# Lane-major q/k columns in fewer, longer loads, and the query mask added in the row-maximum pass

## The reference

```python
x = x + _L0_attn_ref(_layernorm(x), ...)
x = x + _L0_ffn_ref(_layernorm(x), ...)
x = x + _L1_attn_ref(_layernorm(x), ...)
x = x + _L1_ffn_ref(_layernorm(x), ...)
# _L1_attn_ref
q = jnp.einsum('btc,oc->bto', x, Wq).reshape(B, T, H, D)
k = jnp.einsum('btc,oc->bto', x, Wk).reshape(B, T, H, D)
v = jnp.einsum('btc,oc->bto', x, Wv).reshape(B, T, H, D)
att = jnp.einsum('bqhd,bkhd->bhqk', q, k) * SCALE
att = jnp.where(mask[None, None, :, :], -jnp.inf, att)   # mask: j > i
att = jax.nn.softmax(att, axis=-1)
out = jnp.einsum('bhqk,bkhd->bqhd', att, v).reshape(B, T, C)
return jnp.einsum('btc,oc->bto', out, Wo)
```

## Time and profile before

| | us |
|---|---|
| median of 3 runs | 2110.64 |
| range of the runs | 2103.11 to 2110.79 |
| the profiled execution | 2108.77 |
| its span | 2107.0 |

### The profile page before, as it was taken

How to read it: one execution, slowest core, us unless ns; L and a number is a source line. 1 busy time by engine, 2 the same in 40 slices (tenths; PEclk the granted TensorE clock), 3 DMA queues, 4 the chain that set the end, 5 groups by cost and what they waited for, 6 DMA issues and landing times.

```text
span 2107.0 us, 34513 instructions
## 1 busy us (share of the span) xinstructions
PE 1619.2 (77%) x10136; PEld 907.4 (43%) x10136; DVE 1236.6 (59%) x3717; ACT 778.5 (37%) x1387; POOL 501.6 (24%) x487
## 2 busy tenths in 40 slices
PE   3869898979787878888888888798889781137765
PEld 2335454535353434444444444444454441135554
DVE  5456767666667575757575757575766526861111
ACT  1225252525252525252525252525254242134331
POOL 2311212121212121212121212121212002006887
PEclk7879999989899989899989899999999875568897
DMA  2041321313131313130313130404031400024444
GB/s 63 16 50 33 40 50 27 50 26 51 25 52 25 52 24 57 19 59 18 58 18 59 17 61 15 64 12 63 13 58 20 65 7 10 0 39 86 89 89 59
DMA packets 113452, 86.56 MB, mean 41 GB/s; under 512 B 21569, under 2 KB 107841, under 8 KB 113345
## 3 DMA queue, kind: packets, MB, share of 16 engines
q1 hardware_dynamic: 102080, 76.58, 21.4%
q0 software_dynamic: 11264, 8.92, 3.2%
HBM read 58.95 MB, written 25.72 MB: 40 GB/s over the span
## 4 chain that ended last, share of the span: by engine, by line
PE 47%; DVE 17%; issue 17%; POOL 5%; DMA 4%; ACT 4%; SPq 2%; DVEq 1%; ACTq 0%; POOLq 0%
PE ba L580 6%; PE bo L839 5%; PE facc L695 5%; PE fa L669 5%; PE ba L585 5%; PE fa L685 5%; POOL out L552 3%; SPq L330 2%; ACT probs L1015 2%; DVE passed L1460 2%; DVE nm L1263 2%; PE ba L587 2%; PE ba L582 2%; POOL got L522 2%; DMA KT<-qk_parts 1%
## 5 line engine op out<-in xcount | busy, mean ns | idle before, releaser
L585 PE MATMUL ba<-KT,QT 72*128 72x512 bf16 (+3 forms) x1024 | 262.2, 320 | 182.5 <-DVE nm L1263 129.2
L1015 ACT ACTIVATE probs<-ba 128x512 f32<-128x512 f32 x640 | 330.5, 640 | 97.7 <-PE ba L582 96.9
L459 POOL TENSOR_TENSOR hh<-th,gb 128x512 f32<-128x512 f32 x128 | 161.9, 1265 | 697.5 <-ACT gb L971 427.0
L580 PE MATMUL ba<-QT,KT 75*128 75x512 bf16 (+3 forms) x1024 | 253.3, 310 | 35.2 <-ACT probs L1015 28.7
L1263 DVE TENSOR_REDUCE nm<-ba 128x1 f32<-128x512 f32 x256 | 174.6, 682 | 179.5 <-issue 131.2
L585 PEld LDWEIGHTS ba<-KT,QT 72*128 72x128 bf16 x1024 | 105.0, 103 | 344.5 <-DVE nm L1263 155.8
L587 PE MATMUL ba<-mask_q,identb 128*128 128x128 bf16 x1024 | 200.8, 230 | 0.0
L987 ACT ACTIVATE sil<-fa 128x512 f32<-128x512 f32 x160 | 95.4, 596 | 274.9 <-PE fa L669 274.8
L582 PE MATMUL ba<-mask_k,identb 128*128 128x128 bf16 x1024 | 195.5, 224 | 0.0
L669 PE MATMUL fa<-f_nT,w 128*128 128x512 f32 x320 | 187.1, 669 | 1.2 <-ACT sc L1046 1.2
L685 PE MATMUL fa<-f_nT,w 128*128 128x512 f32 x320 | 181.1, 649 | 0.0
(11 more groups left out here) (284 smaller groups left out, 2643.2 us busy)
## 6 DMA issues: line engine op xcount, KB each, us to landing
QT<-qk_parts SPq DMA_DIRECT2D x288, 64.0 KB
KT<-qk_parts SPq DMA_DIRECT2D x288, 64.0 KB
qk_parts<-qkp SPq DMA_DIRECT2D x32, 384.0 KB, 2.5
fc<-in_L_ffn_fc_weight SPq DMA_DIRECT2D x32, 256.0 KB
xin<-in_L_attn_x SPq DMA_DIRECT2D x16, 256.0 KB, 13.4
out<-x SPq DMA_DIRECT2D x16, 256.0 KB, 2.3
xn_rows<-row SPq DMA_DIRECT2D x16, 256.0 KB, 2.4
w<-in_L_w SPq DMA_DIRECT2D x3, 640.0 KB, 6.7
```

The lines of the kernel that those rows point to most:

```text
L459: pool.tensor_tensor(hh[:, e % 2], th[:, e % 2], gb[:, e % 2], ALU.mult).then_inc(S["s_h"], 1)
L580: pe.matmul(bank[:, col:col + w], lhsT=KT[0:K_ROWS, head, blk * P:(blk + 1) * P], rhs=QT[0:K_ROWS, head, blk * P:], start=True, stop=False)
L585: pe.matmul(bank[:, col:col + w], lhsT=QT[0:QK_ROWS, head, blk * P:(blk + 1) * P], rhs=KT[0:QK_ROWS, head, 0:w], start=True, stop=False)
L1015: act.activation(probs[:, pair % 3, f_], ba[n % 3][:], ACT.Exp, scale=SCALE).then_inc(S["s_exp"], 1)
```

## The change

The weights of q and k are copied once into `w_qk` with their columns in lane-major order, d * 16 + h, so that the 16 heads of a lane are neighbours in q, k and `qk_parts`. `qk_parts` gets 5 slots for parts instead of 3; for k, slots 3 and 4 are parts 0 and 1 again, written by one more DMA. The 72 rows of `QT` and `KT` are taken in three shifts of 24: q parts 0, 1, 2 against k parts shift, shift + 1, shift + 2, so one load fills 24 partitions, with a run of 8 heads of 512 tokens, 8 KB, for each. There are 12 loads per batch instead of 36, and the totals that the semaphores wait for are adapted.

`mask_q` becomes 512 wide, zero but for the last 128 columns. The second matmul of a query-major fill goes. VectorE's reductions become `tensor_tensor_reduce`: negated (scores + mask), written back into the PSUM bank, and their minimum, started from 1e38, into `nm`. A fill with two heads takes two such operations instead of one, and each fill's first stands behind a separate wait and no-op (`apart`).

```diff
-        qk_parts = nc.dram_tensor("qk_parts", (BATCH, 2, PARTS, P, SEQ), BF16, kind="Internal").ap()
+        qk_parts = nc.dram_tensor("qk_parts", (BATCH, 2, 2 * PARTS - 1, P, SEQ), BF16, kind="Internal").ap()
...
-                    sp.dma_start(qk_parts[b, w].rearrange("c p t -> p c t"), qkp[:, w]).then_inc(S["s_qkw"], 16)
-                sp.wait_ge(S["s_qkw"], 32 * b + 32)
+                    sp.dma_start(qk_parts[b, w].rearrange("c p t -> p c t")[:, 0:PARTS], qkp[:, w]).then_inc(S["s_qkw"], 16)
+                sp.dma_start(qk_parts[b, 1].rearrange("c p t -> p c t")[:, PARTS:], qkp[:, 1, 0:PARTS - 1]).then_inc(S["s_qkw"], 16)
+                sp.wait_ge(S["s_qkw"], 48 * b + 48)
...
-                for i in range(PARTS):
-                    for j in range(PARTS):
-                        r = (i * PARTS + j) * HD
-                        for t, w, part in ((QT, 0, i), (KT, 1, j)):
-                            sp.dma_start(t[r:r + HD, heads], qk_parts[b, w, part].rearrange("(h d) t -> d h t", d=HD)[:, heads])\
-                              .then_inc(S[f"s_qk{half}"], 16)
+                for shift in range(PARTS):
+                    r = slice(shift * PARTS * HD, (shift + 1) * PARTS * HD)
+                    for t, w, part in ((QT, 0, 0), (KT, 1, shift)):
+                        rows = qk_parts[b, w, part:part + PARTS].rearrange("c (d h) t -> (c d) h t", h=HEADS)
+                        sp.dma_start(t[r, heads], rows[:, heads]).then_inc(S[f"s_qk{half}"], 16)
...
             const(pool.memset(mask_q[:], 0.0))
-            const(pool.affine_select(mask_q[:], mask_q[:], [[-1, P]], ALU.is_ge, MASKED, base=0, channel_multiplier=1))
+            last_ = mask_q[:, SEQ - P:]
+            const(pool.affine_select(last_, last_, [[-1, P]], ALU.is_ge, MASKED, base=0, channel_multiplier=1))
...
-                    pe.matmul(bank[:, col:col + w], lhsT=QT[0:QK_ROWS, head, blk * P:(blk + 1) * P],
-                              rhs=KT[0:QK_ROWS, head, 0:w], start=True, stop=False)
-                    last = pe.matmul(bank[:, col + w - P:col + w], lhsT=identb[:], rhs=mask_q[:], start=False, stop=True)
+                    last = pe.matmul(bank[:, col:col + w], lhsT=QT[0:QK_ROWS, head, blk * P:(blk + 1) * P],
+                                     rhs=KT[0:QK_ROWS, head, 0:w], start=True, stop=True)
...
-                pe.matmul(facc[:], lhsT=w_q1[:], rhs=b_nT[:], start=True, stop=True).then_inc(S["s_q"], 1)
+                pe.matmul(facc[:], lhsT=w_qk[:, 0].rearrange("p d h -> p (d h)"), rhs=b_nT[:], start=True, stop=True).then_inc(S["s_q"], 1)
...
                 dve.wait_ge(S["s_S"], FILLS * b + n + 1)
+                apart(dve)
+
+                def lowest(head, blk, col):
+
+                    w = (blk + 1) * P
+                    return dve.tensor_tensor_reduce(bank[:, col:col + w], bank[:, col:col + w], mask_q[:, SEQ - w:], -1.0, -MASKED, ALU.add, ALU.min,
+                                                    nm[:, blk, head:head + 1])
+
                 if f in (0, 2):
-                    last = dve.tensor_reduce(nm[:, 3, h:h + 1], bank[:], X, ALU.max, negate=True)
+                    last = lowest(h, 3, 0)
                 elif f in (1, 3):
-                    dve.tensor_reduce(nm[:, 2, h:h + 1], bank[:, 0:384], X, ALU.max, negate=True)
-                    last = dve.tensor_reduce(nm[:, 0, h:h + 1], bank[:, 384:512], X, ALU.max, negate=True)
+                    lowest(h, 2, 0)
+                    last = lowest(h, 0, 384)
                 else:
-                    last = dve.tensor_reduce(nm[:, 1, h:h + 2], bank[:].rearrange("p (h k) -> p h k", h=2), X, ALU.max, negate=True)
+                    lowest(h, 1, 0)
+                    last = lowest(h + 1, 1, 256)
...
+                    for w, t in enumerate((w_q1, w_k1)):
+                        dve.tensor_copy(w_qk[:, w], t[:].rearrange("p (h d) -> p d h", d=HD)).then_inc(S["s_wqk"], 1)
```

More of the change, by code:

```diff
@@ L74, in build_kernel @@
         identb = sb("identb", [P, P], BF16)
-        mask_q = sb("mask_q", [P, P], BF16)
         mask_k = sb("mask_k", [P, P], BF16)
@@ L88, in build_kernel @@
         logits_flat = sb("logits", [P, TILES, E1])
+        mask_q = sb1("mask_q", [P, SEQ], BF16)
         w_kvq = sb1("w_kvq", [P, 3 * D])
@@ L104, in build_kernel @@
         w_v1 = sb1("w_v1", [P, D])
+        w_qk = sb1("w_qk", [P, 2, HD, HEADS])
         w_o1 = sb1("w_o1", [P, D])
@@ L243, in build_kernel @@
             s_h1 s_h3 s_gb s_gbc s_sil s_t s_h s_hs s_ym s_yT s_yTt s_x2 s_fc
-            s_pad s_lnb s_varb s_rsb s_T3 s_nT3 s_q s_k s_v s_p1 s_r1 s_p2 s_p3 s_vp s_qkw s_qk0 s_qk1 s_S s_red s_nmp s_nmt
+            s_pad s_wqk s_lnb s_varb s_rsb s_T3 s_nT3 s_q s_k s_v s_p1 s_r1 s_p2 s_p3 s_vp s_qkw s_qk0 s_qk1 s_S s_red s_nmp s_nmt
             s_nmT s_mx0 s_mx1 s_st s_exp s_pv s_oT s_tr s_norm s_aTt s_aT s_wo s_x3 s_row s_T4 s_nT4 s_l1 s_l1c
@@ L700, in r_turn @@
                     pe.wait_ge(S["s_wback"], BW)
+                    pe.wait_ge(S["s_wqk"], 2)
                 pe.wait_ge(S["s_lnb"], r + 1)
@@ L705, in r_q @@
                 pe.wait_ge(S["s_nT3"], r + 1)
-                pe.matmul(facc[:], lhsT=w_q1[:], rhs=b_nT[:], start=True, stop=True).then_inc(S["s_q"], 1)
+                pe.matmul(facc[:], lhsT=w_qk[:, 0].rearrange("p d h -> p (d h)"), rhs=b_nT[:], start=True, stop=True).then_inc(S["s_q"], 1)
             def r_k(r):
                 pe.wait_ge(S["s_r1"], 2 * r + 1)
-                pe.matmul(facc[:], lhsT=w_k1[:], rhs=b_nT[:], start=True, stop=True).then_inc(S["s_k"], 1)
+                pe.matmul(facc[:], lhsT=w_qk[:, 1].rearrange("p d h -> p (d h)"), rhs=b_nT[:], start=True, stop=True).then_inc(S["s_k"], 1)
             def r_v(r):
@@ L759, in fill @@
                     if n == 0:
-                        pe.wait_ge(S["s_qk0"], 16 * 2 * PARTS * PARTS * (b + 1))
+                        pe.wait_ge(S["s_qk0"], 16 * 2 * PARTS * (b + 1))
                         pe.wait_ge(S["s_exp"], FILLS * b)
                     if n == FILLS // 2:
-                        pe.wait_ge(S["s_qk1"], 16 * 2 * PARTS * PARTS * (b + 1))
+                        pe.wait_ge(S["s_qk1"], 16 * 2 * PARTS * (b + 1))
                     if n >= 3:
@@ L1027, in y_phase @@
                 if r is not None:
-                    act.wait_ge(S["s_qkw"], 32 * r)
+                    act.wait_ge(S["s_qkw"], 48 * r)
                     copy(qkp[:, 0, 0], facc[:], "s_q", r + 1, "s_p1")
```

## The result

The changed kernel takes 2020.3 us (2019.0 to 2022.1) where the kernel before took 2106.9 in the same comparison (2095.6 to 2110.8): a ratio of 0.960, 95% interval 0.956 to 0.964. The forecast was 1998, with a range of 1925 to 2080. The profiled executions took 2108.8 and 2019.0 us, 89.8 less; the sum had said 111 less.

What follows compares the result with a forecast made beforehand. It took TensorE to bound the X phase, VectorE close, with VectorE stalled 11.0 us at each jump back. From 2108.8 us, -78 (stall), -21 (open waits) and -12 (X phase) gave 1997.8, put as 1998; range 1925 to 2080.

Steps and rivals of the forecast that it cites:

- The bound before, and where the gain would come from: VectorE stalls 11.0 us after each loop jump back, its code fetch held up by the QT and KT loads.
- The stall, -78 us: VectorE's wait at each of twelve jumps back falls from 11.0 to 4.5 us with faster loads; range -102 to 0.
- waits for the tail of it and for the next `xin`: At the jump back, VectorE's code fetch still waits for the end of half 1's loads and the next input load.
- The open waits, -21 us: Outside the loop, 27 us of TensorE waits for loads mostly go, less 2.8 us for the extra write; range -27 to 0.
- The X phase, -12 us: Bound moves to VectorE at about 46.5 of 47.5 us, -1 us per pass; bounds -4.3 (TensorE bound) to +3.
- Plus 1 to 2 us where it can't work: X phase: added to VectorE's 44.8 us of work, as the phase's end goes through yT on ScalarE and TensorE.
- The half-clock stretch behind the stall: TensorE's clock is 0.50 in the 3 us after the stall; with a shorter stall 1 to 2 us go.
- A: Rival: the jump back costs VectorE some 11 us whatever the DMA does, so the stall stays; 2076 us, chance 0.15.
- B: Rival: the maxima's result costs nothing, TensorE bounds the X phase at -4.3 us, stall 3.5 us; 1940 us, chance 0.17.
- C: Rival: writing into the PSUM bank being read takes VectorE a second cycle per element; 2314 us, chance 0.08.
- D: Rival: long runs are moved no faster, the stall stays, only the X phase gains; 2097 us, chance 0.05.
- The signs: First maximum 3 to 6 us after the last operation, loads well over 100 GB/s, maxima 60 to 100 ns longer, more `nm` waits.

Runs made afterwards that it cites:

- e3: Kernel before with its slow loads, but half 1 issued only once VectorE has ended its first maximum behind the jump back: 2165.8 us, ratio 1.027.
- e7: e1 with each load on 8 partitions again, 36 loads of 64 KB, keeping the 8 KB runs: 2121.3 us, ratio 1.001.
- e11: e1 with each load cut by heads into three, so 36 loads on 24 partitions, runs of 2 to 3 KB: 1976.9 us, ratio 0.936.
- e1: Changed kernel's new loads alone, with the row maxima and mask matmul of the kernel before: 1978.7 us, ratio 0.938.
- e8: Changed kernel with plain reductions and no mask matmul, the mask of the query-major scores left out altogether: 1969.9 us, ratio 0.930.
- e2: Changed kernel's new maxima, without the mask matmul, with the old loads of the kernel before: 2156.1 us, ratio 1.021.
- e12: Kernel before with VectorE's loop written out as straight code, its 36 slow loads untouched: 2026.9 us, ratio 0.959.
- e4: Changed kernel with VectorE's loop alone written out as straight code, other engines keeping their loops: 1943.5 us, ratio 0.921.
- e5: e1 with VectorE's loop written out as straight code: 1924.1 us, ratio 0.907.
- e6: e1 with rows of qk_parts 64 bytes apart in DRAM, so 12 loads on 24 partitions but runs of 1 KB: 1991.6 us, ratio 0.939.
- e10: e5 with the loop written out as straight code for TensorE, ScalarE and GpSimd too, SyncE keeping its loop: 1913.0 us, ratio 0.905.

## Why the prediction came out as it did

**The bound before, and where the gain would come from:** right. The piece at the jump back was the largest thing to win, and it was the loads (e3, e7, e11).

**The stall, -78 us:** right mechanism, 16 us short; it gave -94. The rate of 160 GB/s was what the windows show (162), the six issues took 2.3 us for the 2.5 assumed. The step that was mis-sized is the last, "waits for the tail of it and for the next `xin`", 2 us on top of a bare fetch. In e1, whose half 1 is issued 8.2 us ahead of the jump as in before, the last long packet is through 0.2 us behind it, the fetch starts at 1.1, and the stall is 3.1; loads and `xin` hold it up by 0.3 at most. The bare fetch, bounded at 2.5, is 2.8 to 2.9 (e8, e3).

**The open waits, -21 us:** -27 by e1 (17.9 and 9.2), of which 2 are in e2 and e12 as well, whose slow loads can't explain them: the first write to `qk_parts` comes at 94.9 us for 96.8. The 2.8 us taken for one more write were wrong in kind: the 5.66 us of two issues are mostly SyncE's wait for `s_p3`, and the third write took 0.37.

```profile
860.67 5.65 SPq L314 DMA_DIRECT2D qk_parts<-qkp  x2
866.50 0.37 SPq L315 DMA_DIRECT2D qk_parts<-qkp  x1
```

**The X phase, -12 us:** this is the step that failed. All that isn't in the two terms above came to +31.5 us (-89.8 + 94.2 + 27.1), a miss of 43. VectorE's own sum, 44.8 us forecast and 44.9 in the window, came out by luck: over the whole phase before VectorE was busy 41.3 us, not 39.3, and the new maxima added 3.4, not 5.5 (a result costs 0.03 to 0.05 us, not 0.07). Three things around it were wrong.
- "Plus 1 to 2 us where it can't work" was 5.5: VectorE is idle that much in the 50.4 us. 2.0 us of it are the wait at the phase's end that was foreseen, and 2.1 are three waits for fills. Fill and maximum alternate through three banks, and that a phase so close to both engines' work is bound by their exchange before it is bound by either is argued from this, not shown. TensorE's side looks alike: with VectorE at its old cost, e8, 2.7 us less of matmuls gave 1.3, not the 4.3 of the bound.
- The X phase of before was 49.8 us by its own marks, not the 47.5 that the sum measured against; the window of 47 us, to which 47.5 is near, left out its first 1.4 and last us (49.3 in that pass, VectorE 41.3):

```profile
954.58:1003.91 49.33, 46.90 (x226) 24.06 (x227) 41.30 (x107) 13.20 (x23) 14.36 (x12) 0.95 0.03 8
```

- The Y phase, at which the sum didn't look, lost 1.5 us per pass to TensorE's clock.
And the batches outside the loop, where the prediction took nothing, lost 6.9 us (0.6 and 6.3).

**The half-clock stretch behind the stall:** that some of it goes was right in kind, but not the size. The time at a granted clock of 0.50 within the X phase fell from 5.4 to 4.1 us per pass, some 0.6 us of work by half of the difference, where 1 to 2 were put down. It went in full only with the stall (e4, e5).

**The rivals.** A (the stall stays) is refuted by e3. B (cheap maxima) fell twice: the result costs 0.03 to 0.05 us per operation, and even plain reductions with no mask bring only 9 us. C (a second cycle per element) isn't there: 1.04 ns. D's "long runs are moved no faster" was nearly true of the runs, as e7 and e6 show (60 GB/s in 8 KB runs; 146 and 164 for 1 and 8 KB), but the loads grew wider as well. The sign and the range held since the stall was much the largest term; that the sum missed by only 22 us is partly luck, as the loads gave 22 more than their two terms and the rest 43 less.

**The signs.** The first maximum comes 3.25 us after the last operation, the loads move 162 GB/s, and TensorE's waits for `nm` in an X phase, the stall's apart, are 2.7 us for 1.0, as foretold. The maxima take 30 to 50 ns more by starts, not 60 to 100.

## What to carry to other kernels

A load that filled 8 partitions was slow here however long its runs were, and it held up what shared the DMA engines with it: code fetches at jumps, and the next input. Make loads wide first, and write out the loop of the engine whose idle time at the jump shows as "issue". Where two engines alternated through three banks and both were near their limit, moving work from one to the other cost some three quarters of what it added and returned half of what it took; price both ends of such a move by a kernel that leaves the work out. When a stall is removed, look in the same queue for the next wait that it had covered (`xin` here).

The best kernel here is e10, 1913 us, with the loads of the change, the maxima of before and straight code: 0.905 of before, where the whole change gave 0.960.

## What the hardware showed that was not expected

- An 8 KB packet into 8 partitions took 0.95 us and into 24 partitions 0.63; at 8 partitions the DMA engines were 49 to 65% busy and yet no instruction packet started for 8 us.
- A jump back of VectorE cost 2.7 to 3.0 us with an idle DMA (e3), and about 4.8 between e1 and e5 (57.6 us for twelve). ScalarE and GpSimd, whose bodies of the same loop have 164 and 53 rows in the trace for VectorE's 441, went on 0.1 to 0.2 us after theirs.
- `tensor_tensor_reduce` from PSUM into the same PSUM bank runs at 1.04 ns per element, with a fixed cost of 0.085 to 0.115 us by starts; its accumulator read of 0.141 us runs beside the next operation.
- Taking 64 short matmuls from the X phase came with a TensorE at 1.2 GHz (granted 0.50) for 3.4 us, some 36 us into the Y phase, in two of three passes of the kernels with VectorE's loop. The cause is open, and with straight code the counts don't divide so.
